# One graph-attention layer and a top-2 expert layer: GpSimd's 104 gather groups of the edge stream written out, without their loop

## What is computed

```python
h = layernorm(x)                                   # 3125 x 256
h_s, z = h @ W_self.T, h @ W_func.T
e = leaky_relu(concat(z[src], z[dst], w) @ W_att.T, 0.01)
alpha = softmax of e over the edges of one destination
agg = segment_sum(alpha * z[src], dst)
h_new = relu(where(deg > 0, h_s + agg, h));  x = x + (h + h_new)
f = layernorm(x)                                   # then 8 experts, top 2
gates = top-2 of softmax(f @ router_w.T), normalised
y_e = (silu(f @ w1_e.T) * (f @ w3_e.T)) @ w2_e.T;  x = x + sum_e gates_e * y_e
```

## Time and profile before

| | us |
|---|---|
| median of three runs | 1161.75 |
| the profiled execution, its own time | 1163.98 |
| span of its instructions | 1162.2 |
| TensorE busy (matmul) | 875.9 |
| GpSimd busy | 618.8 |
| ScalarE busy | 591.3 |
| VectorE busy | 582.2 |
| first row gather starts | 71.1 |
| last row gather starts | 615.6 |

### The profile page before, as it was taken

One profiled execution on the slowest core, in us unless ns is written; L12 is line 12 of the kernel. 1 busy time (PEld: TensorE's weight loads), 2 busy tenths in 40 slices (PEclk: granted clock), 3 DMA queues, 4 the chain that ended last, 5 costly groups with the idle time before them and its releaser, 6 DMA issues.

```text
span 1162.2 us, 20301 instructions
## 1 busy us (share of the span) xinstructions
PE 875.9 (75%) x4358; PEld 718.8 (62%) x4359; DVE 582.2 (50%) x1860; ACT 591.3 (51%) x1514; POOL 618.8 (53%) x616
## 2 busy tenths in 40 slices
PE   5969575766767767767767720599989999999995
PEld 5713353545645645645556510598978889898995
DVE  7503344544544545444544339455555555555553
ACT  4400757777687787786877721124233333333331
POOL 2047777777777677676761003435455354545442
PEclk9979887877778777876867855699999999999998
DMA  9549544545545545454542142043232322222221
GB/s 275 143 172 364 188 120 120 147 131 135 143 121 138 133 127 139 127 134 124 151 122 70 37 171 79 19 114 103 46 103 45 104 37 37 36 38 36 37 41 23
DMA packets 76385, 128.76 MB, mean 111 GB/s; under 512 B 21085, under 2 KB 56418, under 8 KB 75186
## 3 DMA queue, kind: packets, MB, share of 16 engines
q0 software_dynamic: 30720, 69.90, 26.1%
q1 hardware_dynamic: 38393, 51.59, 13.6%
q10 hardware_dynamic: 7200, 6.56, 1.7%
HBM read 106.86 MB, written 17.86 MB: 107 GB/s over the span
## 4 chain that ended last, share of the span: by engine, by line
PE 57%; issue 13%; DVE 6%; POOL 2%; DMA 2%; ACT 1%; POOLq 1%; DVEq 0%; ACTq 0%; SPq 0%
PE bank L1268 15%; PE bank L1196 15%; PE bank L1307 6%; PE bank L1133 4%; PE bank L1135 4%; PE bank L1168 3%; PE bank L1314 3%; PE bank L1297 2%; PE bank L1064 2%; DMA xg<-ttab,row_ix 2%; PE bank L1179 1%; PE bank L1148 1%; POOL out_rows L815 1%; POOL row_ix L821 1%; ACT split_w L525 1%
## 5 line engine op out<-in xcount | busy, mean ns | idle before, releaser
L767 POOL DMA_INDIRECT early<-ztab,early x416 | 400.0, 961 | 207.6 <-issue 123.3
L1268 PE MATMUL bank<-split_w,operands 128*128 x1344 | 243.4, 331 | 3.4 <-issue 2.1
L1268 PEld LDWEIGHTS bank<-split_w,operands 128*128 128x128 f32 x1344 | 220.1, 195 | 8.0 <-issue 5.6
L1196 PE MATMUL bank<-early,W 128*128 128x258 f32 x832 | 224.2, 417 | 0.0
L1196 PEld LDWEIGHTS bank<-early,W 128*128 128x128 f32 x832 | 165.0, 209 | 32.0 <-issue 8.2
L964 ACT ACTIVATE W<-early 128x128 f32<-128x128 f32 x416 | 170.8, 482 | 19.5 <-PE bank L1196 14.4
L815 POOL DMA_INDIRECT out_rows<-late,row_ix x56 | 89.0, 1589 | 166.0 <-DVE late L1809 119.0
L1133 PE MATMUL bank<-wself_sb,early 128*128 128x256 f32 x100 | 49.6, 651 | 109.2 <-issue 103.6
L953 ACT ACTIVATE early<-iota_row,W 128x128 f32<-128x128 f32 x416 | 131.6, 388 | 0.0
L1033 ACT ACTIVATE late<-bank 128x384 f32<-128x384 f32 x56 | 27.5, 491 | 204.5 <-PE bank L1268 204.5
L1133 PEld LDWEIGHTS bank<-wself_sb,early 128*128 128x128 f32 x100 | 28.5, 314 | 122.2 <-issue 117.9
(11 more groups left out here) (230 smaller groups left out, 1431.3 us busy)
## 6 DMA issues: line engine op xcount, KB each, us to landing
W<-in_experts SPq DMA_DIRECT2D x8, 2132.0 KB, 9.0
W<-in_wt SPq DMA_DIRECT2D x26, 512.0 KB, 6.6
early<-ztab,early POOLq DMA_INDIRECT x416, 2.8
early<-in_x SPq DMA_DIRECT2D x26, 128.0 KB, 2.1
ztab<-early SPq DMA_DIRECT2D x25, 129.0 KB, 6.3
early<-ztab SPq DMA_DIRECT2D x25, 128.0 KB
early<-late SPq DMA_DIRECT2D x25, 128.0 KB
out_rows<-early ACTq DMA_DIRECT2D x25, 128.0 KB, 2.3
```

The costliest lines, as they stand in the source:

```text
L767: nc.gpsimd.indirect_dma_start(out=zg[:, k * KG + c, :], out_offset=None, in_=ztab, in_offset=bass.IndirectOffsetOnAxis(ap=src_here[:, k / ...
L1196: last = mm(ps[2 + k // 2 % 2][:, 0:ZR], prob_hot[:, k % 3, c * P:(c + 1) * P], zg[:, k * KG + c, :], start=(k % 2 == 0 and c == 0), stop= ...
L1268: last = mm(bank[:, 0:n], x[:, (k % 2 * KC + c) * P:(k % 2 * KC + c + 1) * P], split_w[:, bass.ds(at + (part + w + c * H), n)], start=(i = ...
```

## The change

The `peel` argument of the one `run` call for the gathers becomes 104 // 12 = 8, which is the number of full rounds, so that no loop is emitted: all 104 groups are written out. The groups, their order, their semaphores and the wait values are the same; the wait values are constants throughout. No other engine's program changes. GpSimd's program gets longer by 48 groups of instructions.

```diff
-                run(pool, GROUPS, AHEAD, PEEL, [(0, gather)])
+                run(pool, GROUPS, AHEAD, GROUPS // AHEAD, [(0, gather)])
```

## The result

| | before | changed |
|---|---|---|
| median of 20 runs each, us | 1161.70 | 1160.06 |
| lowest to highest, us | 1148.76 to 1168.02 | 1138.42 to 1165.40 |
| ratio of the two medians | | 0.9986 |
| ratio as the comparison gives it, 95% interval | | 0.9889 [0.9850, 0.9929] |
| profiled execution, its own time, us | 1163.98 | 1165.40 |

The two ratios differ because the comparison keeps only executions within 1.5% of the shortest one of the same kernel: the changed kernel's shortest is 1138.42 us, so only five of its 20 stay (1138.42, 1148.46, 1148.99, 1149.37, 1151.58), against 19 of 20 of the kernel before. The other 15 lie from 1156.66 to 1165.40 us, like the kernel before. So the question is not where 1.1% went in every execution, but where five short ones come from.

The account below looks back on a forecast made before the run. TensorE's node work was taken as late after 262 us, with GpSimd having time over; removed, added and moved code sum to 0 + 0 + 0, so the median stays at 1161.7 us, range 1158.1 to 1164.2.

Parts of the forecast that it names:

- rival 1: Gather stream: GpSimd's sequencer is on the path after all, so all 3.7 us come back, giving 1158.1 us; chance 0.05.
- The cost of the edges and register operations: GpSimd's sequencer in the gather loop: 2.1 us plus 1.6 us, together 3.7 us, hidden under waits, so worth 0.
- The added code: GpSimd's program: 48 more groups, 240 instructions to fetch; taken as 0, at most 0.1 us for a stall at the worst place.
- the gaps of 0.30 us: Between GpSimd's gathers at line 767: expected to stay 0.30 us, as a sign that the forecast is right.
- The slack of 6 us behind L1495: VectorE behind a ring wait: 1.2 us before it takes the rows plus 4.8 us idle before L1438 absorb late gathers.
- Rival 2: Experts' loop on GpSimd: moved code stalls at each edge, up to 2.5 us in each of six rounds, 1176.5 us; chance 0.06.
- pause of over 3.6 us: POOLq behind line 482 or 541 after 738 us: the sign that moved code stalls the experts' loop, with TensorE waiting.
- GpSimd's wait for L1196: Gather stream after 262 us: GpSimd still waits about 20 us for TensorE at the same groups if the forecast holds.
- the dearer figure: GpSimd's loop branches: the Trainium skill's about 108 ns per compare-and-branch, making edges 0.3 us dearer in all, still under cover.
- The 0.35 us of an edge: GpSimd's sequencer, from the increment to the end of the first wait's register operation; five edges and an entry make 2.1 us.
- How the numbers follow: Closing odds on the median: faster 0.07, same 0.85, slower 0.08, with about 0.2% (2.3 us) taken as what can be told.
- the chance of 0.03: Odds on the measured median: 0.03 that it falls beyond 2.3 us on the fast side by scatter alone.

Follow-up runs that it names:

- e2: The changed kernel repeated with the same diff, against the kernel before: 1162.03 us, ratio 1.0012 [0.9993, 1.0032].
- e8: The changed kernel repeated on a chip where the kernel before takes 1336.17 us: 1335.59 us, ratio 1.0004 [0.9978, 1.0030].
- e12: The changed kernel repeated on a third chip, where the kernel before takes 1337.62 us: 1334.74 us, ratio 0.9966 [0.9929, 1.0002].
- e13: The changed kernel once more, against the kernel before at 1338.86 us: 1336.70 us, ratio 0.9981 [0.9945, 1.0018].
- e1: The kernel before, unedited, compared with itself: 1159.2 us, ratio 0.9974 [0.9952, 0.9997].
- e7: The kernel before, unedited, against itself on a chip where it takes 1336.17 us: 1338.94 us, ratio 1.0008 [0.9976, 1.0039].
- e14: The kernel before, unedited, against itself at 1338.86 us: 1336.51 us, ratio 1.0000 [0.9967, 1.0032].
- e4: Kernel before, with each of the loop's 60 groups raising held(pool)'s semaphore eleven times instead of once: 1160.83 us, ratio 0.9998 [0.9969, 1.0027].
- e3: Kernel before, with only the first round of gathers written out instead of three, so the loop runs seven rounds: 1160.21 us, ratio 1.0032 [0.9947, 1.0116].
- e11: Kernel before, with thirty-one semaphore steps per loop group instead of one, on a third chip: 1333.43 us, ratio 0.9953 [0.9921, 0.9985].
- e15: Kernel before (1338.86 us), with an extra 128x256 multiply on GpSimd per group: 1297.23 us, ratio 0.9709 [0.9643, 0.9775].
- e9: Kernel before (1337.62 us, a third chip), with an extra 128x256 multiply on GpSimd per group: 1299.91 us, ratio 0.9696 [0.9639, 0.9753].
- e10: Changed kernel with an extra 128x256 multiply on GpSimd per group, against the kernel before at 1337.62 us: 1297.94 us, ratio 0.9686 [0.9618, 0.9754].
- e16: Changed kernel with an extra 128x256 multiply on GpSimd per group, against the kernel before at 1338.86 us: 1297.84 us, ratio 0.9684 [0.9617, 0.9752].

## Why the prediction was right, and where it was wrong

**Ratios together.** Changed over before by medians of all executions: 0.9986, 1.0012, 0.9996, 0.9978, 0.9984 (first comparison, e2, e8, e12, e13), mean 0.9991. The unchanged kernel over itself: 0.9988, 1.0021, 0.9982 (e1, e7, e14), mean 0.9997. The two can't be told apart: they lie 0.06% apart, and ratios of the unchanged kernel to itself range over 0.4%. Taken alone these times can't exclude rival 1's 0.3% either; that is done by the traces and by e4. The 0.9889 did not come back in four repetitions.

**What was right.** The median of 1160.06 us lies 1.6 us from the forecast, as near as the unchanged kernel comes to itself. The cost of the edges and register operations: 0 as predicted, and e4 makes it more than an argument, since 13 times as much sequencer work cost nothing either. The added code: 0; the gaps of 0.30 us, the 544 us from first to last gather and the unmoved 4.89 us of TensorE are the signs that the prediction named. The slack of 6 us behind L1495: e4 used up to 1.9 us of it, in eleven places, and the stream got no longer; the rest of it wasn't tried. Rival 1 falls: its 3.7 us would have shown as a shorter way from first to last gather, which changed by 0.4 us. Rival 2 falls: at the experts' five loop edges the sequencer's next row starts 0.25 to 0.28 us behind the branch in both kernels, and the stage keeps its length. (The pause of over 3.6 us that I had named as its sign was no good sign: behind line 541 pauses of up to 4.4 us stand in both kernels, before a wait.) One sign I had announced was misread in advance: GpSimd's wait for L1196 "of about 20 us" shows as 5.2, because the label went over to "issue"; only the sum of the two stayed. And one row was read too quickly: 40 to 58 ns is the length of the branch's own row, but the next instruction of the sequencer starts 150 to 180 ns after the branch's start where it jumps, and 90 ns where it falls through. So the rows don't decide against the dearer figure that stands beside them in the prediction. The 0.35 us of an edge, which the sum used, holds all of it.

**What was wrong.** The step at fault is the one under "How the numbers follow": that about 0.2% (2.3 us) is what a measurement can tell from no change, and the chance of 0.03 for a gain beyond it "by scatter alone", both taken from three runs that spanned 2.5 us. Three runs can't show the scatter. The median of all executions fell by 1.6 us, within those 2.3; but the ratio of the executions that the comparison keeps fell by 1.1%, some 13 us, and that ratio of the unchanged kernel to itself (e1) is off by 0.26%. 20 runs of the kernel before span 19 us, and executions of 1138 to 1154 us occur beside the usual 1156 to 1168, with a granted clock (where it is recorded) of 0.857 to 0.874 instead of 0.845 to 0.855. In the comparisons with the short stream, the executions under 1155 us (none lies between 1154.1 and 1155.8) were:

| kernel | short | of |
|---|---|---|
| before, first comparison | 2 | 20 |
| changed, first comparison | 5 | 20 |
| before, beside e1 to e4 | 4 | 35 |
| before again (e1) | 3 | 12 |
| changed again (e2) | 0 | 12 |
| more loop (e3) | 3 | 12 |
| eleven steps (e4) | 1 | 12 |

The changed kernel has 5 of 32, one in 6.4, and the kernels with a loop 13 of 91, one in 7. (Counted under 1152 us it is 5 of 32 against 7 of 91; if all had the same chance, the changed kernel would get five or more of those twelve once in six times, 0.17, worked out from the counts. Without the first comparison, which raised the question, it is 0 of 12 against 11 of 71.) So short executions come with the loop as well as without it, and that the first comparison drew five was, as far as the counts can tell, luck. They don't exclude a weak tie to the change. What makes an execution short is open: none of them was caught in a profile, only their clock is known, and whether it is the cause isn't.

The term for scatter was mis-sized, not the mechanism: I should have set the chance of a measured gain without a real one by the spread of single executions, and by the fact that a comparison of a kernel with itself (e1) can exclude 1.

## What to carry to other kernels

Before a loop on an engine's sequencer is written out, look at what the engine behind it does across an edge: where the gaps between its instructions stay the same and the sequencer next stands at a wait, the edge cost nothing here, and neither did ten times its work. When a result contradicts a profile that has hardly changed, look at the single executions and run the unchanged kernel against itself before looking for a mechanism. And read a wait in a trace by the length of the idle time, not by its label alone: the same wait moved from "PE bank L1196" to "issue" when two waits came to stand in one instruction.

## What was not expected of the hardware

**The stream can take 165 to 182 us longer on another chip.** First comparison and e1 to e4: 544 us from first to last gather. The later ones, on two other chips than e1 to e4: 709 to 726 us for the same two kernels (e7 70.3 to 796.1), while the experts' stage keeps its length (from 419 to 426 us in both). Whether it is the chip or the time of the run isn't separated, as no chip shows both lengths. In the same two kernels one place stands out in the trace: VectorE's L1533, which reads what TensorE's L1187 wrote. In e1 and then in e7, in order of time:

```profile
403.79 0.29 PE L1187 MATMUL bank<-early,mirror 128*128 128x16 f32 x2
...
404.18 0.17 DVE L1533 TENSOR_TENSOR early<-early,bank 128x16 f32<-128x16 f32 x1 [0.37 <-PE bank L1187]
```
```profile
404.24 0.40 PE L1187 MATMUL bank<-early,mirror 128*128 128x16 f32 x2 [0.17 <-ACT early L940]
...
408.53 0.95 POOL L767 DMA_INDIRECT early<-ztab,early  x1 [0.30 <-issue]
411.28 0.17 DVE L1533 TENSOR_TENSOR early<-early,bank 128x16 f32<-128x16 f32 x1 [7.63 <-remote]
411.94 0.95 POOL L767 DMA_INDIRECT early<-ztab,early  x1 [2.46 <-remote]
```

From L1187's start to L1533's it is 0.4 us in the one and 7.0 in the other, and GpSimd's next gather, which waits for TensorE too, starts 0.7 us later. Over the stream, what ended VectorE's idle time before L1533, in the changed kernel of the first comparison and in e8:

```profile
  PE bank L1187: 10.2, 11
```
```profile
  remote: 104.0, 15
  PE bank L1187: 6.5, 4
```

In e8 100 of its 165 us more stand in this one wait. In e7's example no engine has a row from 409.5 to 411.3 us, and the semaphore events of L1187, L1064 and L1196, three steps of TensorE, all come between 411.1 and 411.3 us. Matmul ends in the trace are modelled, so TensorE may have been at work longer than its rows say; why on these chips and not on the other is open. The lost time isn't tied to this wait, though. In e11 the same step (L1535) hardly waits:

```profile
  PE bank L1189: 7.1, 5
```

and the stream is as long as in e12 all the same; there VectorE waits 196.8 us for rows instead. So the late rows of e11 take the place of another wait and don't come on top. What bounds the long stream isn't shown.

**More work can shorten it.** With the extra multiply on GpSimd, e15's stream is 672.4 us (69.7 to 742.1), 40 us less than the 711.9 of the unchanged kernel beside it (e14), and the waits before VectorE's same step (L1538 in e15) are 66.4 + 11.2 us instead of e14's 106.7 + 10.1:

```profile
  remote: 66.4, 14
  PE bank L1192: 11.2, 4
```

In e9 that step still waits 90.8 + 11.8 us, with a stream of 685.1 us, so this wait isn't where all of the gain lies. e9, e10, e15 and e16 all show the gain of about 3%, on one chip; on a chip with a short stream it wasn't tried. The granted clock of the span is 0.83 in e15 and 0.82 in e14. Why more work on GpSimd shortens the stream is not shown.

**Where the stream is short, its rounds keep their length.** In all six profiles with the short stream (both kernels twice, e3, e4) 12 groups take 64.7 to 64.9 us on average from group 36 to 72 (single rounds 64.1 to 65.2), and nothing done to GpSimd's program moved that average by more than 0.2 us.
